# A mixture-of-experts stage whose second-layer weights are loaded from another engine's queue

## The chip, the core and the metric

The kernel runs on one core of a Trainium2 chip. The time is the device time of one execution in microseconds (us), on that core. The engines are named as in the profile: PE is TensorE (matmuls), PEld its weight loads, DVE VectorE, ACT ScalarE, POOL GpSimd, SP SyncE. A "q" behind a name means the engine's instruction queue. Any engine that issues a DMA only starts it; the bytes are moved by the core's 16 DMA engines.

## The reference, cut to what matters

Four layers follow each other on x of shape (16, 256, 256), each added to its input: attention, a gated recurrence, a mixture of four experts with a shared expert, and a recurrent net with tanh. The change touches the third alone:

```python
gate_scores = jax.nn.softmax(gate_logits, axis=-1)          # (16, 4), from means of x and the condition
topk_w, topk_i = jax.lax.top_k(gate_scores, 2)              # two experts for each of 16 images
...
for e in range(E):
    h = jax.nn.gelu(context_c @ ew1[e] + eb1[e], approximate=True)     # 256 -> 1024
    y = h @ ew2[e] + eb2[e]                                            # 1024 -> 256
    out = out + w_be[:, e][:, None, None] * mask[e][None, :, None] * y
shared = jax.nn.gelu(context_c @ sw1 + sb1, approximate=True) @ sw2 + sb2
```

## The kernel before

The kernel runs its stages one after the other, each a block with a program for every engine and a barrier at its end. During attention all expert weights are split into a high and a low part (matmuls in a fast fp32 format need both) and written to a buffer in HBM, `weight_halves` (`halves` in the code). There an expert has a 2 MB half for the first layer (w1) and one for the second (w2), laid out so that each of the 128 partitions reads one run of 16 KB.

The expert stage (`experts`, from L931) computes only what is chosen: two experts for each of 16 images are `JOBS` = 32 jobs. VectorE works out the choice, and writes the experts' numbers to the tile `which` (L1076). A job `n` has eight ticks (`FC` = 8), one for each 128 of the 1024 hidden columns. In a tick TensorE does an "up" (L1184 to L1186, six matmuls with w1 into `ph`), ScalarE the GELU (L1023), VectorE splits the result into a high part (L1131) and a low part (L1133), and two ticks later TensorE does the "down" (L1200 to L1202, six matmuls with w2 into `py`). The ups and downs are interleaved as up(t), down(t-2); a job has 96 matmuls of 256 columns.

The weights lie in two buffers each, used in turn (`n % 2`), with a semaphore for each buffer in `w_in`. The order is set by waits written by hand:

- SP reads the expert's number into a register, waits until the downs of job n-2 are done (`down_done`), and issues both loads of job n, w1 first (L950). They stand in one DMA queue.
- TensorE waits for w1 of job n before its first up (L1179) and for w2 before its first down (L1193), which comes two ticks later.
- After the last job but one SP also loads the shared expert's weights, as job 32, for the next stage. That stage (`shared_and_rnn`) begins on POOL with three memsets (L1407, L1408, L1410); TensorE waits for the last of them and for both loads (L1341) before L1296.

POOL writes a few small tables at the start of the expert stage and then waits at its end.

Of the kernel before, what the change touches and what calls it, by code (L numbers as in the profile page):

```python
# [18 lines left out]
NE, F = 4, 1024  # L19
FC = F // P  # L20
# [80 lines left out]
def build(nc, x_tok, x_dm, small_in, mod_w, w_qkv, w_out, w_fih, ew1, ew2, sw1, sw2, wx, wh, out):  # L101
# [13 lines left out]
    with hold:  # L115
        XT = sb(hold, "XT", [P, DC, B, T])
        small = sb(hold, "small", [P, SMALL_W])
        ident = sb(hold, "ident", [P, P])
        silu = sb(hold, "silu", [P, DC, B])
        eps8 = sb(hold, "eps8", [P, 1])  # L120
        wx_sb = sb(hold, "wx_sb", [P, DC, D])
        wh_sb = sb(hold, "wh_sb", [P, DC, D])
        later_loaded = sem(hold, "later_loaded")
        pieces_out = [sem(hold, f"pieces_out{q}") for q in range(2)]
        halves = nc.dram_tensor("weight_halves", (NE + 1, 2, P, 2, DC * F), fp32).ap()

        def vec(name, a=None, z=None):
            at = SMALL_AT[name]
            width = dict(SMALL)[name]
            return small[:, at + (a or 0):at + (width if z is None else z)]  # L130

        with ExitStack() as early:
            wfih_sb = sb(early, "wfih_sb", [P, DC, 3 * D])
            attention(nc, locals())
            recurrence(nc, locals())
        experts(nc, locals())
# [790 lines left out]
PIECES = 8 * (NE + 1)  # L927
# [3 lines left out]
def experts(nc, env):  # L931
    fp32, fp32r, ALU, ACT, AX = (env[k] for k in ("fp32", "fp32r", "ALU", "ACT", "AX"))
    sb, ps, sem, vec = (env[k] for k in ("sb", "ps", "sem", "vec"))
    XT, silu, halves = (env[k] for k in ("XT", "silu", "halves"))
    int32 = mybir.dt.int32
    JOBS = TOP * B
# [3 lines left out]
    with st:  # L940
        xhi = sb(st, "xhi", [P, DC, B, T], fp32r)
        xlo = sb(st, "xlo", [P, DC, B, T], fp32r)
        w1 = sb(st, "w1", [P, 2, 2, DC, F], fp32r)
        w2 = sb(st, "w2", [P, 2, 2, FC, D], fp32r)
        w_in = [[sem(st, f"w{w}_in{q}") for q in range(2)] for w in (1, 2)]

        def load_weights(sp, n, src):

            for w, dst, form in ((0, w1, "p v c f -> p (v c f)"), (1, w2, "p v c d -> p (v c d)")):
                sp.dma_start(dst[:, n % 2].bitcast(fp32).rearrange(form), src[:, w].rearrange("o p v n -> p (o v n)"))\  # L950
                    .then_inc(w_in[w][n % 2], 16)

        with ExitStack() as routed:
            g = sb(routed, "g", [P, RING, T])
# [18 lines left out]
            which = sb(routed, "which", [P, JOBS], int32)  # L973
# [8 lines left out]
            up_done, gelu_done, hi_done, lo_done, down_done, y_added, y_part = (sem(routed, n) for n in (  # L982
                "up_done", "gelu_done", "hi_done", "lo_done", "down_done", "y_added", "y_part"))
            gate_in, gate_mm, exp_in, exp_done, tables, chosen_ready, b1_ready, x_hi, x_split, biased = (
                sem(routed, n) for n in ("gate_in", "gate_mm", "exp_in", "exp_done", "tables", "chosen_ready", "b1_ready", "x_hi",
                                         "x_split", "biased"))
# [2 lines left out]

            @block.sync  # L990
            def _(sp):
                for q in range(2):
                    sp.wait_ge(env["pieces_out"][q], 16 * (PIECES // 2))
                sp.wait_ge(chosen_ready, 1)
                for n in range(JOBS):
                    e = sp.value_load(which[0:1, n:n + 1], min_val=0, max_val=NE - 1)
                    if n >= 2:
                        sp.wait_ge(down_done, FC * (n - 1))
                    load_weights(sp, n, halves[bass.ds(e, 1)])
                sp.wait_ge(down_done, FC * (JOBS - 1))  # L1000
                load_weights(sp, JOBS, halves[NE:NE + 1])

            @block.gpsimd
            def _(pool):
                nc.gpsimd.memset(ones[:], 1.0).then_inc(tables, 1)
                nc.gpsimd.memset(earlier[:], 0.0).then_inc(tables, 1)
                for e in range(NE):
                    nc.gpsimd.memset(number[:, e:e + 1], float(e)).then_inc(tables, 1)
                pool.wait_ge(tables, 2 + NE)
                for e in range(1, NE):  # L1010
                    nc.gpsimd.memset(earlier[:, e, 0:e], 1.0).then_inc(tables, 1)

            @block.scalar
            def _(act):
# [473 lines left out]
```

## Time and profile before

| | |
|---|---|
| Median of 3 runs | 1654.78 us (1653.81 to 1656.48) |
| The profiled execution | 1659.2 us |
| Its span, first to last instruction | 1657.6 us |
| Busy share of the span: PE, PEld, DVE, ACT, POOL | 79%, 62%, 52%, 39%, 20% |
| Weight loads `w<-weight_halves` | 66 of 2048 KB, median 12.0 us from issue to landing |
| Granted TensorE clock, mean | 0.890 of 2.4 GHz |

The profile is of one execution. A view by windows gives each engine's busy time within a stretch; "DMA share" is the mean busy share of the 16 DMA engines. In the timeline a row has its start and length, the engine, the line, the operation and its tiles, and in brackets how long the engine stood idle before it and what the profile takes to have ended that. A DMA's row on SP is only the issue; "DMA to landing" tells how long after the issue its data were there. "Issue" as a cause means that the profile shows nothing that the engine waited for.

### The profile page before, as it was taken

To read this page: it belongs to the slowest core of one execution; us is meant where nothing else is said; L and a number is where in the kernel's file an instruction comes from. 1 tells how busy PE (TensorE), PEld (TensorE's weight loads), DVE (VectorE), ACT (ScalarE), POOL (GpSimd) and SP (SyncE) were. 2 spreads that over 40 slices of the span, in tenths; PEclk is the share of its full clock that TensorE was granted. 3 is DMA by queue.
4 is the path that set the end of the run, shared out by engine and by line. 5 is a ranking of instruction groups with operands and counts; after the bars stand their busy time and mean duration, and the time that the engine had idled before them with its cause. 6 is when DMAs were issued, how large, how long until landed. Compare 5 with 4: busy or idle time off the path is not lost. (4 is left out here: it accounts for less than half of the span.)

```text
span 1657.6 us, 37130 instructions
## 1 busy us (share of the span) xinstructions
PE 1313.8 (79%) x15240; PEld 1035.8 (62%) x15240; DVE 855.8 (52%) x1946; ACT 645.3 (39%) x1205; POOL 324.6 (20%) x311
## 2 busy tenths in 40 slices
PE   2378887887888755445149999999998999999997
PEld 2245655655656422112049999999998888888885
DVE  3656556556555245555565565655654334433432
ACT  1155565565554445544413233323322233223332
POOL 2252342442433134444300000000000000000000
PEclk8589898898897887777559999999999999999998
DMA  8112112112112300000047888888883000000000
GB/s 320 53 39 78 39 38 77 38 39 77 39 39 77 102 0 0 0 0 0 0 203 305 340 347 334 340 353 326 345 335 125 9 16 15 16 10 16 16 15 16
DMA packets 37880, 188.06 MB, mean 113 GB/s; under 512 B 3056, under 2 KB 13424, under 8 KB 29040
## 3 DMA queue, kind: packets, MB, share of 16 engines
q1 hardware_dynamic: 37744, 186.10, 29.4%
q8 instruction: 103, 1.69, 0.4%
q14 instruction: 33, 0.27, 0.1%
HBM read 160.66 MB, written 25.17 MB: 112 GB/s over the span
## 5 line engine op out<-in xcount | busy, mean ns | idle before, releaser
L1023 ACT ACTIVATE g<-ph,b 128x256 f32<-128x256 f32 x256 | 121.5, 475 | 276.5 <-PE ph L1186 276.4
L813 PE MATMUL pg<-XT,wfih_sb 128*128 x192 | 117.6, 777 | 102.8 <-DVE logs L898 101.0
L546 DVE TENSOR_REDUCE mx<-pR 128x4 f32<-128x1024 f32 x128 | 155.6, 1222 | 70.9 <-PE pR L673 69.6
L1376 DVE STREAM_TRANSPOSE preT<-pr 128x64 f32<-128x64 f32 x256 | 64.1, 250 | 223.8 <-PE pr L1274 223.8
L1200 PE MATMUL py<-ghi,w 128*128 128x256 f32 x512 | 147.5, 288 | 20.5 <-issue 16.2
L437 ACT ACTIVATE probs<-pR 128x1024 f32<-128x1024 f32 x128 | 131.7, 1030 | 77.0 <-PE pR L682 76.8
L1184 PE MATMUL ph<-xhi,w 128*128 128x256 f32 x512 | 146.5, 286 | 17.9 <-DMA w<-weight_halves 17.9
L1131 DVE CAST ghi<-g 128x256 fp32r<-128x256 f32 x256 | 74.8, 292 | 156.8 <-ACT g L1023 156.6
L813 PEld LDWEIGHTS pg<-XT,wfih_sb 128*128 128x128 f32 x192 | 47.4, 257 | 172.8 <-issue 172.8
L1350 ACT ACTIVATE hs<-preT 128x32 f32<-128x32 f32 x256 | 58.8, 230 | 228.6 <-DVE preT L1376 228.6
L1185 PE MATMUL ph<-xlo,w 128*128 128x256 f32 x512 | 146.0, 285 | 0.0
L1186 PE MATMUL ph<-xhi,w 128*128 128x256 f32 x512 | 145.9, 285 | 0.0
L1201 PE MATMUL py<-glo,w 128*128 128x256 f32 x512 | 145.3, 284 | 0.0
L1202 PE MATMUL py<-ghi,w 128*128 128x256 f32 x512 | 145.3, 284 | 0.0
L1274 PE MATMUL pr<-wh_sb,hs 128*32 128x64 f32 x4096 | 112.1, 228 | 15.5 <-ACT hs L1350 15.5
L1200 PEld LDWEIGHTS py<-ghi,w 128*128 128x128 f32 x512 | 98.6, 192 | 25.3 <-DVE glo L1133 14.0
L1133 DVE TENSOR_TENSOR glo<-g,ghi 128x256 fp32r<-128x256 f32 x256 | 109.0, 426 | 8.8
L1184 PEld LDWEIGHTS ph<-xhi,w 128*128 128x128 f32 x512 | 99.4, 194 | 18.9 <-issue 17.2
L673 PE MATMUL pR<-KT,QT 48*128 48x256 f32 x512 | 62.1, 332 | 57.1 <-DVE mx L546 56.8
L1274 PEld LDWEIGHTS pr<-wh_sb,hs 128*32 128x32 f32 x4096 | 70.1, 110 | 50.6 <-ACT hs L1350 20.9
L1186 PEld LDWEIGHTS ph<-xhi,w 128*128 128x128 f32 x512 | 99.4, 194 | 0.0
L1185 PEld LDWEIGHTS ph<-xlo,w 128*128 128x128 f32 x512 | 99.4, 194 | 0.0
(189 smaller groups left out, 3006.5 us busy)
## 6 DMA issues: line engine op xcount, KB each, us to landing
w<-weight_halves SPq DMA_DIRECT2D x66, 2048.0 KB, 12.0
weight_halves<-wparts SPq DMA_DIRECT2D x40, 512.0 KB, 4.0
modw<-in_ew SPq DMA_DIRECT2D x32, 256.0 KB, 4.3
xn<-in_x_tok SPq DMA_DIRECT2D x4, 1024.0 KB, 12.0
XT<-in_x_dm SPq DMA_DIRECT2D x2, 2048.0 KB, 14.0
out_dm<-staged SPq DMA_DIRECT2D x16, 256.0 KB, 2.1
modw<-in_sw SPq DMA_DIRECT2D x8, 256.0 KB, 4.2
modw<-in_mod_w SPq DMA_DIRECT2D x1, 768.0 KB, 7.4
```

What stands on the lines that cost most here:

```text
L437: nc.scalar.activation(probs[:, j % 4], pR[k][:], ACT.Exp, scale=HD ** -0.5).then_inc(free[k], 1)
L546: nc.vector.reduce_max(mx[:, :, 2 * j:2 * j + 2].rearrange("p t s -> p s t"), pR[k][:].rearrange("p s (t k) -> p s t k", t=TC), AX.X).then ...
L813: i = nc.tensor.matmul(pg[u][:, g], wfih[:, c, g * D + u * P:g * D + (u + 1) * P], XT[:, c, bass.ds(2 * p, 2)], start=(c == 0), stop=(c == ...
L1023: nc.scalar.activation(g[:, t % RING], ph[t % RING][:, 0:T], ACT.Gelu_apprx_tanh, bias=b1[:, n, f:f + 1]).then_inc(gelu_done, 1)
L1133: nc.vector.tensor_tensor(glo[:, t % RING], g[:, t % RING], ghi[:, t % RING].bitcast(fp32), ALU.subtract).then_inc(lo_done, 1)
L1184: nc.tensor.matmul(dst, whi, hi, start=(k == 0), stop=False)
L1185: nc.tensor.matmul(dst, whi, lo, start=False, stop=False)
L1186: i = nc.tensor.matmul(dst, wlo, hi, start=False, stop=(k == DC - 1))
L1200: nc.tensor.matmul(dst, whi, hi, start=(f == 0), stop=False)
L1201: nc.tensor.matmul(dst, whi, lo, start=False, stop=False)
L1202: i = nc.tensor.matmul(dst, wlo, hi, start=False, stop=(f == FC - 1))
L1274: i = nc.tensor.matmul(dst[QW * j:QW * (j + 1)], prev[:, c], quad(wh[:, c], j), start=False, stop=(c == DC - 1), skip_group_check=True)
```

## The change

`load_weights` loads one of the two layers, and a new helper `load_all` holds the loop that SP had. SP calls it for w1, POOL for w2, behind its small tables. Each of the two engines waits for the stored halves and for the choice, reads the expert's number for each job and waits for `down_done` with the same values as before. The semaphores that TensorE waits for are the same.

```diff
-        def load_weights(sp, n, src):
-            for w, dst, form in ((0, w1, "p v c f -> p (v c f)"), (1, w2, "p v c d -> p (v c d)")):
-                sp.dma_start(dst[:, n % 2].bitcast(fp32).rearrange(form), src[:, w].rearrange("o p v n -> p (o v n)"))\
-                    .then_inc(w_in[w][n % 2], 16)
+        def load_weights(eng, n, src, w):
+            dst, form = ((w1, "p v c f -> p (v c f)"), (w2, "p v c d -> p (v c d)"))[w]
+            eng.dma_start(dst[:, n % 2].bitcast(fp32).rearrange(form), src[:, w].rearrange("o p v n -> p (o v n)"))\
+                .then_inc(w_in[w][n % 2], 16)
+
+        def load_all(eng, w, which, chosen_ready, down_done):
+            for q in range(2):
+                eng.wait_ge(env["pieces_out"][q], 16 * (PIECES // 2))
+            eng.wait_ge(chosen_ready, 1)
+            for n in range(JOBS):
+                e = eng.value_load(which[0:1, n:n + 1], min_val=0, max_val=NE - 1)
+                if n >= 2:
+                    eng.wait_ge(down_done, FC * (n - 1))
+                load_weights(eng, n, halves[bass.ds(e, 1)], w)
+            eng.wait_ge(down_done, FC * (JOBS - 1))
+            load_weights(eng, JOBS, halves[NE:NE + 1], w)
...
             @block.sync
             def _(sp):
-                for q in range(2):
-                    sp.wait_ge(env["pieces_out"][q], 16 * (PIECES // 2))
-                sp.wait_ge(chosen_ready, 1)
-                for n in range(JOBS):
-                    e = sp.value_load(which[0:1, n:n + 1], min_val=0, max_val=NE - 1)
-                    if n >= 2:
-                        sp.wait_ge(down_done, FC * (n - 1))
-                    load_weights(sp, n, halves[bass.ds(e, 1)])
-                sp.wait_ge(down_done, FC * (JOBS - 1))
-                load_weights(sp, JOBS, halves[NE:NE + 1])
+                load_all(sp, 0, which, chosen_ready, down_done)
...
             @block.gpsimd
             def _(pool):
...
+                load_all(pool, 1, which, chosen_ready, down_done)
```

## Rows read from the trace of the kernel before

**Rows 1.** Window: us; busy of PE, PEld, DVE, ACT, POOL; clock, DMA share, GB/s.

```profile
873.40:1246.40 373.00, 351.63 (x2882) 346.86 (x2880) 220.66 (x643) 114.00 (x240) 0.00 (x0) 1.00 0.85 339
```

**Rows 2.** Timeline of SP's queue: first and last weight loads of the steady part.

```profile
873.37 0.85 SPq L950 DMA_DIRECT2D w<-weight_halves  x2
...
1246.35 0.34 SPq L950 DMA_DIRECT2D w<-weight_halves  x1
```

**Rows 3.** Timeline of TensorE within a job.

```profile
1226.01 0.28 PE L1184 MATMUL ph<-xhi,w 128*128 128x256 f32 x1
1226.13 0.28 PE L1185 MATMUL ph<-xlo,w 128*128 128x256 f32 x1
```

**Rows 4.** Waits from 873.4 to 1246.4 us: total us, times, longest.

```profile
PE py L1200 <- issue: 15.6, 19, 1.3
...
PE ph L1184 <- DMA w<-weight_halves: 2.5, 3, 1.4
```

**Rows 5.** Timeline and landing (L950): job 13's w1, its w2, TensorE's next start.

```profile
1010.44 0.34 SPq L950 DMA_DIRECT2D w<-weight_halves  x1
...
DMA to landing us min/median/max: 7.7/7.7/7.7
...
1010.96 0.33 SPq L950 DMA_DIRECT2D w<-weight_halves  x1
...
DMA to landing us min/median/max: 12.1/12.1/12.1
...
1023.13 0.35 PE L1200 MATMUL py<-ghi,w 128*128 128x256 f32 x1 [0.64 <-issue]
```

**Rows 6.** Windows in and after the body of a job's loads.

```profile
1013.50:1022.00 8.50, 8.50 (x74) 8.50 (x73) 6.62 (x21) 2.85 (x6) 0.00 (x0) 1.00 0.99 422
1022.00:1024.50 2.50, 1.86 (x16) 1.69 (x15) 1.08 (x3) 0.47 (x1) 0.00 (x0) 1.00 0.67 164
```

**Rows 7.** Timeline and landing (L950): job 30's w1, TensorE's stop, the next issue.

```profile
1220.59 0.34 SPq L950 DMA_DIRECT2D w<-weight_halves  x1
...
DMA to landing us min/median/max: 9.7/9.7/9.7
...
1228.77 0.28 PE L1202 MATMUL py<-ghi,w 128*128 128x256 f32 x1
1230.47 0.35 PE L1184 MATMUL ph<-xhi,w 128*128 128x256 f32 x1 [1.42 <-DMA w<-weight_halves]
...
1233.75 0.85 SPq L950 DMA_DIRECT2D w<-weight_halves  x2
```

**Rows 8.** Timeline of POOL around the stage.

```profile
1258.77 1.80 POOL L1407 MEMSET hs<- 128x2048 f32 x1 [433.51 <-POOLq L953]
```

**Rows 9.** DMA transfers from 873.4 to 1246.4 us.

```profile
DMA packets 8673, 126.29 MB, mean 339 GB/s; under 512 B 959, under 2 KB 959, under 8 KB 959
```

**Rows 10.** Timeline of TensorE before the last stage, and the window after it.

```profile
1260.90 0.58 PE L1296 MATMUL phs<-xhi,w 128*128 128x256 f32 x1 [3.45 <-POOL row L1410]
1261.28 0.42 PE L1298 MATMUL phs<-xlo,w 128*128 128x256 f32 x1
1261.49 0.41 PE L1300 MATMUL phs<-xhi,w 128*128 128x256 f32 x1
...
1260.12:1266.92 6.80, 6.02 (x28) 6.02 (x29) 2.34 (x7) 1.43 (x3) 0.67 (x3) 0.50 0.00 0
```

**Rows 11.** Landing (L950) and timeline: job 0's w1 and the first matmul.

```profile
L950 SPq DMA_DIRECT2D w<-weight_halves x1: 378/378/378, 846.7 to 846.7; - x1
...
DMA to landing us min/median/max: 7.9/7.9/7.9
...
854.70 0.55 PE L1184 MATMUL ph<-xhi,w 128*128 128x256 f32 x1 [15.33 <-DMA w<-weight_halves]
```

**Rows 12.** The page, part 5: VectorE's two operations on the hidden layer.

```profile
L1131 DVE CAST ghi<-g 128x256 fp32r<-128x256 f32 x256 | 74.8, 292 | 156.8 <-ACT g L1023 156.6
...
L1133 DVE TENSOR_TENSOR glo<-g,ghi 128x256 fp32r<-128x256 f32 x256 | 109.0, 426 | 8.8
```

## The prediction

> **What bounds the kernel now.** I read the span by stages first. The expert stage, from the first weight load at 846.7 us [rows 11] to the end of the last expert at about 1257 us, is the only one that the change touches; its steady part alone is 373.00 us [rows 1]. In that stretch TensorE is busy 351.63 us, the clock is granted in full, GpSimd does nothing and the 16 DMA engines are busy 0.85 of the time at 339 GB/s. Two resources are therefore near their limit at once, and what counts is which one is late at which point.
>
> The queue of SP says how long one job (one chosen expert of one image) takes: the loads for job 2 are issued at 873.37 us, those for the shared expert, which stand in as job 32, at 1246.35 us [rows 2]. That is 30 periods in 372.98 us, 12.43 us each. A job has 96 matmuls, one every 0.12 us [rows 3], so TensorE needs 11.52 us; the other 0.91 us, 27 us over the stage, is waiting. The list of waits shows where: before L1200, the first matmul that reads the second layer's weights (w2), 15.6 us in 19 stops are put down to "issue"; before L1184, which reads the first layer's (w1), a DMA costs 2.5 us in 3 stops [rows 4].
>
> One job shows what "issue" hides. Its w1 load is issued at 1010.44 and lands 7.7 us later; its w2 load is issued 0.52 us behind it and lands after 12.1 us, thus at 1023.04. TensorE stands idle and goes on at 1023.13 [rows 5], 0.09 us after the landing, though ScalarE and VectorE had nothing left to deliver for that matmul (the page names an engine because it has no better candidate). So **w2's landing is what is late now, by about one microsecond in a typical job, and w1's is not, or hardly**. The reason that w1 is early is order: both loads stand in one queue, so w1's 2 MB go through the DMA engines first. In the body of a load the engines are busy 0.99 of the time at 422 GB/s [rows 6]: they are full, and 2.10 MB take 4.97 us there. The difference of the two landings, 1023.04 less 1018.14, is 4.9 us, the same thing.
>
> **When is each load due?** The job in which w1 was late gives this without arithmetic on ticks. Its load was issued at 1220.59 and took 9.7 us, to 1230.3. TensorE's last matmul before the stop began at 1228.77; the next could have begun at 1228.89, 8.3 us after the issue. It began at 1230.47, and the next pair of loads went out at 1233.75 [rows 7], 3.4 us after the landing, since 24 matmuls and the semaphore stand between them. So when w1 decides, the period is w1's time to landing plus 3.4 us, and it decides from 8.1 us on (8.1 + 3.4 = 11.5). w2 is due 30 matmuls, 3.6 us, after w1's point: at 11.9 us after the issue.
>
> **The change, part by part.**
>
> (a) Removed from SP: one of two DMA issues per job (0.34 us) and its address registers. SP only waits between them, so this is worth nothing by itself. The SP queue holds nothing else in this stage.
>
> (b) Added to POOL: three waits, 32 reads of the expert's number, 33 DMA issues. POOL is idle from 825 to 1258 us [rows 8], and the read stands ahead of the wait for L1202, as on SP. Behind the load loop on POOL stand only the block's end and the memset L1407; the last load goes out near 1246.35 and L1407 starts at 1258.77, when the other engines have reached the block's end, so 12 us cover it. Cost zero; without that cover it would be once the issue, below 1 us.
>
> (c) Moved: w2's transfer leaves the queue in which it stood behind w1's. Both sets of 2.10 MB now ask for the same 16 DMA engines at almost the same time. Nothing in this trace has two bulk queues active at once, nor any DMA issued by POOL, so I bound the delay of w1. Lower end zero: POOL's load starts only when w1's is through, or yields to it. Upper end 4.9 us: w2 goes wholly ahead. If the engines serve both queues in turn, w1 waits for as many of w2's packets as it has itself left when these begin to come: 4.9 us less POOL's extra start-up. The nearest row for a start-up is the 0.52 us between two issues on SP; POOL may need two or three times that. The packets of this stage are 16.4 KB each [rows 9], so a load is 8 packets on each engine, 0.6 us apiece; who comes last in a turn is half of one, 0.3 us. With 1 us of start-up the delay is 4.9 - 1.0 - 0.3, about 3.5 us. I take that: it lies nearest to the row for a start-up, and nothing in the trace gives either side precedence. w1's own time is 7.7 us in the typical job and 9.7 in the late one [rows 5, 7]; I take 8.0 as an average. So w1 lands after 11.5 us.
>
> The Trainium skill says the same of the engines ("DMA: Bandwidth & Descriptors", Queues, rings and completion order): each serves in turn the queues that hold work for it, a packet at a time. No row of before can show it; by that rule alone the sum is the one I make. The same page gives software-generated DMAs from GpSimd a first byte after about 1 us against 0.6 us for SP's; with their difference of 0.4 us as start-up the delay would be, as an estimate, 4.2 us, and the sum 21 us higher.
>
> (d) Period by w1: 11.5 + 3.4 = 14.9 us. The stop before L1184 is then 3.4 us long in every job, where TensorE stands idle. w2, landing after some 12.6 us as now (the engines have the same bytes to move), is due 14.9 + 0.7 us after the issue and is no longer late.
>
> (e) The clock. A stop of TensorE that ends at 1260.90 us, 3.45 us idle, is followed by a granted clock of 0.50, the 1.2 GHz level, for 6.8 us, with matmuls 0.21 us apart [rows 10]; the stop of 1.42 us at 1230.47 did not lower it [rows 7], since the steady part's mean is 1.00 [rows 1]. The new stops are as long as the first. If the clock is down for all 24 matmuls between w1's landing and the next issue, the period grows by 24 x (0.213 - 0.12) = 2.2 us; if never, by zero. Slow matmuls elsewhere in the job only shorten the stop. I take the middle, 1.1 us: the fall comes some way into or after the stop, so that it covers part of those 24.
>
> (f) Start and end. w1 of job 0 goes out at 846.71, lands 7.9 us later and releases TensorE at 854.70 [rows 11]. It now shares with w2 of job 0: +3.5 us, less the 0.5 us for which job 1 waited for w2. End: the last stage waits for both loads of the shared expert, issued at 1246.35, but it starts at 1260.90 behind L1407 and L1410 [rows 8, 10], 14.5 us after the issue; both land within 12.9 us. Zero.
>
> **Sum.** Period 11.5 + 3.4 + 1.1 = 16.0 us against 12.43: 3.57 x 30 = 107 us. With 3 us at the start: +110 us. The profiled execution took 1659.2 us (span 1657.6), 4.4 us above the median of the three timed runs, 1654.78; the sum is a difference, so I put it on the median: **1765 us, 6.6% slower**.
>
> **A second rule, against the change.** The cast L1131 takes 0.29 us for 256 elements, the two-input L1133 0.42 us [rows 12], so the cast is the quicker of the two at one size. The Trainium skill ("SBUF — State Buffer", the "DVE blocks DMA" trap) says that while VectorE runs a copy in its two-port mode, as casts of this kind are, GpSimd can't write descriptors for its DMAs. No row here shows it. As an estimate it would start w2 up to 0.29 us later and let w1 keep that much more of the engines: up to 9 us less than the sum, in the direction of rival 1.
>
> **The rivals.**
>
> 1. *w1 keeps its lead, w2 is late instead* (18%). If POOL's start-up is long (3 us and more) or its queue yields, w1 is hardly delayed and every microsecond by which w2 lands later than its present 12.6 us is paid directly. For: POOL generates nothing in this trace, so its start-up is unbounded by rows. Against: it would have to be six times SP's 0.52 us. With 0.5 to 1.5 us on each of 30 jobs (15 to 45 us): 1670 to 1700 us.
>
> 2. *w2 goes ahead of w1* (13%). Delay 4.9 us and w1 at 12.9 us: period 16.3 without and 18.5 us with the full loss of clock: +116 to +182 us, with 5 us at the start 1775 to 1842 us.
>
> 3. *Faster* (4%). Two queues keep the engines busy across the gap between jobs, where they were only 0.67 busy [rows 6], and w2 lands by 11.9 us while w1 still lands by 8.1. That removes the 0.91 us: 1627 us. It decides from the point where 4.19 MB land within 11.9 us; at 422 GB/s they take 9.9 us, and a load's own latency is 7.7 - 4.9 = 2.8 us, 12.7 together. So the gap would have to yield 0.8 us.
>
> 4. *No change* (4%): SP's queue is served first and w2's packets follow at once from the other, as they did behind w1 in one queue, so that w2 lands at 12.6 us as before. 1655 us.
>
> The forecast case has 61%, with its own range from 1705 (delay 2.5 us, period 13.9 and little loss of clock: +45 us and 2 to start, raised by a fall now and then) to 1815 us (delay 4.2 and the full 2.2 us).
>
> **How the numbers follow.** Below 1670 lie rivals 3 and 4, 8%; above 1825 the upper third of rival 2, 4%. The range leaves out these 12%: 1670 to 1825. A difference under 0.2% (3.3 us, about what can be told from no change here) comes from rival 4: 4%. Faster 4%, slower 92%.
>
> **What the new profile would show.** Right: a stop before L1184 in nearly every job, by DMA, 3 us long, some 100 us in all; the stops before L1200 gone; issues near 16 us apart; w1 landing after 11 to 12 us and w2 close behind; the granted clock of 873 to the stage's end between 0.75 and 0.95; DMA share down to about 0.66 (0.85 x 12.43 / 16.0). Wrong: w1 still landing within 8.5 us (rival 1, 3 or 4, told apart by w2's landing); w1 landing last (rival 2); or a clock of 1.00 in spite of the stops, which would take (e), 33 us, out of the sum and leave 1732 us.

## The result and the profile after

The changed kernel takes 1734.28 us (median of 4 runs, 1732.15 to 1738.73), the kernel before 1654.30 us beside it (1653.65 to 1656.48). The ratio is 1.0485, with an interval of 1.0459 to 1.0510: slower by 80 us. The profiled execution took 1732.15 us with a span of 1730.5 us, 72.9 us more than the span of before; the rest of the 80 is how the single runs lie (the profiled one is the fastest of the changed kernel, and the profiled one of the kernel before, 1659.2 us, lies above its four timed runs).

The windows of the expert stage first: from the first to the last load of its steady part, from there to the next stage, and one stretch of 3.3 us inside. The columns are those of [rows 1].

```profile
875.60:1316.20 440.60, 368.13 (x2882) 362.92 (x2881) 221.31 (x643) 113.69 (x240) 15.84 (x30) 0.96 0.72 287
1316.20:1332.00 15.80, 10.17 (x84) 9.84 (x82) 6.60 (x20) 2.84 (x6) 1.19 (x2) 0.88 0.68 267
1068.95:1072.25 3.30, 3.30 (x17) 3.30 (x17) 1.41 (x4) 0.73 (x2) 0.00 (x0) 0.50 0.00 0
```

The steady part has grown from 373.0 to 440.6 us. The engines of DMA are less busy (0.72 for 0.85) and move 287 instead of 339 GB/s: the same bytes in more time, with pauses. The clock, 1.00 before, is 0.96, since stretches like the one at 1068.95 ran at 0.50, the 1.2 GHz level. The period follows from the queue of SP, as in [rows 2]:

```profile
875.56 0.34 SPq L950 DMA_DIRECT2D w<-weight_halves  x1
...
1316.15 0.34 SPq L950 DMA_DIRECT2D w<-weight_halves  x1
```

(1316.15 - 875.56) / 30 = 14.69 us, against 12.43. Who waits now (total us, times, longest)?

```profile
POOL w L950 <- PE py L1206: 436.7, 30, 27.2
...
PE ph L1188 <- DMA w<-weight_halves: 72.5, 30, 3.9
```

What answers to [rows 4] has turned round: the stops before the matmul that reads w2 are gone from the list, and there is one of 2.4 us in each of the 30 jobs before L1188, which reads w1 and was L1184. The landings of both loads over the steady part (minimum, median, maximum after the issue):

```profile
L950 SPq DMA_DIRECT2D w<-weight_halves x31: 337/338/347, 875.6 to 1316.1; - x31
...
DMA to landing us min/median/max: 10.0/10.5/12.2
...
L950 POOL DMA_DIRECT2D w<-weight_halves x31: 527/527/530, 876.0 to 1316.4; - x31
...
DMA to landing us min/median/max: 12.0/12.5/13.6
```

w1, which came 7.7 us after its issue in the typical job of [rows 5], now takes 10.5. The mean over the 30 loads, from the records of their landings, is 10.77 us, and 8.14 before. w2 is as late after w1's issue as it was, 13.2 us (13.4 before). One job in detail, by the timeline:

```profile
1113.38 0.34 SPq L950 DMA_DIRECT2D w<-weight_halves  x1
...
1113.86 0.53 POOL L950 DMA_DIRECT2D w<-weight_halves  x1 [13.03 <-PE py L1206]
...
1121.56 0.28 PE L1206 MATMUL py<-ghi,w 128*128 128x256 f32 x1
1123.64 0.35 PE L1188 MATMUL ph<-xhi,w 128*128 128x256 f32 x1 [1.81 <-DMA w<-weight_halves]
...
1126.92 0.34 SPq L950 DMA_DIRECT2D w<-weight_halves  x1
```

w1 goes out at 1113.38 and lands 10.1 us later, at 1123.5; TensorE, free since 1121.83, goes on 0.1 us after that, and the next load goes out 3.4 us after the landing, as in [rows 7]. Which queue moved data in that job is in the view of the DMA queues (packets, MB, share of the 16 engines), read for three stretches: 0 to 4 us after the issue, 4.6 to 8.6 us, 10.1 to 12.6 us.

```profile
q1 hardware_dynamic: 59, 0.97, 75.8%
...
q0 software_dynamic: 54, 0.88, 51.6%
q1 hardware_dynamic: 54, 0.88, 51.6%
...
q0 software_dynamic: 52, 0.59, 55.4%
```

First SP's queue q1 alone (POOL's q0 has no row there), then 54 packets from each, then POOL's alone. The engines take turns packet by packet, and a 16 KB packet takes 0.61 us, as before. By the packet records of 30 jobs, POOL's first packet moves 3.6 us after SP's first, and SP's load has started 75 of its 128 packets by then. The first 16 of a load take 1.29 us each in the mean in both kernels, the later ones 0.61: so these 75 are what 3.6 us hold, and not the 94 that they would hold at the later pace. At the stage's end the barrier's drains are new:

```profile
L965 POOLq DRAIN  x1: 14694/14694/14694, 1316.4 to 1316.4; - x1
...
L965 DVEq DRAIN  x1: 1031/1031/1031, 1326.4 to 1326.4; - x1
```

POOL's queue drains for 14.69 us, from 1316.4 to 1331.1, while VectorE is through at 1327.45. L1411 (L1407 before) must wait for that, and TensorE stands idle for 7.10 us instead of the 3.45 of [rows 10]:

```profile
1331.34 1.80 POOL L1411 MEMSET hs<- 128x2048 f32 x1 [14.39 <-POOLq L965]
...
1333.47 0.58 PE L1300 MATMUL phs<-xhi,w 128*128 128x256 f32 x1 [7.10 <-POOL row L1414]
```

The next stage thus starts 17.3 us after the last issue, 14.5 before. The difference of the spans is accounted for: 2.2 us up to the loads of job 2, 67.6 us in 30 periods, 2.8 us at the stage's end and 0.3 us after it, together 72.9.

### The profile page after: what moved, and what is told of

Same layout as the page of the kernel before. It is cut to its first block and busy times, and to the rows that moved or that the text cites. A ratio compares the mean times of both kernels' runs of the same rounds, so it can differ in the third digit from the quotient of the medians.

```text
span 1730.5 us, 37229 instructions
## 1 busy us (share of the span) xinstructions
PE 1331.9 (77%) x15240; PEld 1050.8 (61%) x15240; DVE 856.2 (49%) x1946; ACT 644.6 (37%) x1205; POOL 342.0 (20%) x344
## 3 DMA queue, kind: packets, MB, share of 16 engines
q1 hardware_dynamic: 32992, 116.90, 18.7%
## 5 line engine op out<-in xcount | busy, mean ns | idle before, releaser
L1188 PE MATMUL ph<-xhi,w 128*128 128x256 f32 x512 | 152.4, 298 | 90.2 <-DMA w<-weight_halves 90.2
L1188 PEld LDWEIGHTS ph<-xhi,w 128*128 128x128 f32 x512 | 103.5, 202 | 95.7 <-issue 95.7
L1204 PE MATMUL py<-ghi,w 128*128 128x256 f32 x512 | 148.9, 291 | 2.1 <-DMA w<-weight_halves 1.1
L1190 PE MATMUL ph<-xhi,w 128*128 128x256 f32 x512 | 148.8, 291 | 0.0
L1206 PE MATMUL py<-ghi,w 128*128 128x256 f32 x512 | 148.7, 290 | 0.0
L950 POOL DMA_DIRECT2D w<-weight_halves x33 | 17.7, 535 | 474.2 <-PE py L1206 451.7
L1189 PEld LDWEIGHTS ph<-xlo,w 128*128 128x128 f32 x512 | 103.4, 202 | 0.0
L1190 PEld LDWEIGHTS ph<-xhi,w 128*128 128x128 f32 x512 | 102.8, 201 | 0.0
## 6 DMA issues: line engine op xcount, KB each, us to landing
w<-weight_halves SPq DMA_DIRECT2D x33, 2048.0 KB, 10.5
XT<-in_x_dm SPq DMA_DIRECT2D x2, 2048.0 KB, 13.8
```

Source lines behind the costliest of these rows:

```text
L1188: nc.tensor.matmul(dst, whi, hi, start=(k == 0), stop=False)
L1189: nc.tensor.matmul(dst, whi, lo, start=False, stop=False)
L1190: i = nc.tensor.matmul(dst, wlo, hi, start=False, stop=(k == DC - 1))
L1204: nc.tensor.matmul(dst, whi, hi, start=(f == 0), stop=False)
L1206: i = nc.tensor.matmul(dst, wlo, hi, start=False, stop=(f == FC - 1))
```

## The experiments

Two theories stood against each other after this. **S**: two transfers that are in the engines together take turns, so that the one that is needed first is late, and how late depends on the head start. **P**: a DMA from POOL is itself the cost, whoever shares with it. The ratios are those to the kernel before, run beside each.

| kernel | median us | ratio (interval) | period us | w1 lands, mean us | w1's landing to next issue, mean us | clock in the steady part |
|---|---|---|---|---|---|---|
| before | 1654.30 | 1 | 12.43 | 8.14 | 4.29 | 1.00 |
| changed | 1734.28 | 1.0485 (1.0459 to 1.0510) | 14.69 | 10.77 | 3.92 | 0.96 |
| held_2 | 1676.51 | 1.0123 (1.0097 to 1.0148) | 12.96 | 8.34 | 4.62 | 0.99 |
| both_pool | 1672.43 | 1.0110 (1.0093 to 1.0127) | 12.72 | 8.29 | 4.43 | 1.00 |
| act_queue | 1837.43 | 1.1098 (1.1080 to 1.1117) | 18.34 | 13.08 | 5.26 | 0.86 |
| swapped | 1843.58 | 1.1140 (1.1122 to 1.1159) | 18.32 | 12.60 | 5.72 | 0.86 |
| sp_later | 1866.10 | 1.1266 (1.1233 to 1.1299) | 19.28 | 12.41 | 6.87 | 0.85 |
| warm | 1710.49 | 1.0328 (1.0312 to 1.0344) | 14.08 | 10.67 | 3.41 | 1.00 |
| last_on_sp | 1727.38 | 1.0440 (1.0419 to 1.0461) | 14.45 | 10.67 | 3.78 | 0.97 |
| early_sp | 1627.72 | 0.9824 (0.9811 to 0.9838) | 11.55 | 8.09 | | 1.00 |
| early_two | 1636.63 | 0.9886 (0.9866 to 0.9906) | 11.64 | 10.24 | | 1.00 |

The last three columns and the period are over jobs 2 to 31 of the profiled execution, from its records; w1's landing and the time from it to the next issue add up to the period (where w2 is late, its stop lies in the second). In `swapped` the second also holds the 0.47 us by which POOL's issue comes behind SP's, in `sp_later` the tick by which SP waits longer. In the two last kernels w1's load no longer waits for the same event, so that column says nothing there.

**held_2: the overlap taken away, POOL kept.**

```diff
+        held = 2
...
                 if n >= 2:
-                    eng.wait_ge(down_done, FC * (n - 1))
+                    eng.wait_ge(down_done, FC * (n - 1) + held * w)
...
-            eng.wait_ge(down_done, FC * (JOBS - 1))
+            eng.wait_ge(down_done, FC * (JOBS - 1) + held * w)
```

> The changed kernel, but POOL issues each w2 load two ticks (about 2.9 us) later than w1's. Theory S (the two transfers take turns on the DMA engines, and w1 is late by the time in which w2's packets come between its own): w2's packets begin when w1's are nearly through, so w1 lands after about 8.2 us instead of 10.8, w2 at about 13 us after w1's issue, the stop before L1188 all but vanishes, the period is 12.5 to 12.9 us, and the time 1655 to 1672 us. Theory P (a DMA from POOL is itself the cost, by software descriptors or slower packets, whoever shares with it): no gain or a loss, 1735 us or more, since w2 only starts later.

Measured: 1676.51 us. w1's landings as in the view above:

```profile
L950 SPq DMA_DIRECT2D w<-weight_halves x31: 337/338/347, 875.2 to 1264.0; - x31
...
DMA to landing us min/median/max: 7.6/7.8/12.2
```

Their median is 7.8 us, and 58 us of the 80 are gone with w2 issued 4.45 us after w1 in the mean. That is more than the two ticks, since TensorE's stop for w2 lies between them. P falls as the main cause. The time is 4 us above what I expected of S: w2 lands 14.1 us after w1's issue and is now itself late, and the next stage starts only 18.7 us after the last issue of w1, since the last w2 goes out 3.8 us after it and POOL's drain waits for its landing.

**both_pool: POOL's queue alone.** `load_all` issues both layers, w1 first, on POOL; SP has none.

```diff
-        def load_all(eng, w, which, chosen_ready, down_done):
+        def load_all(eng, ws, which, chosen_ready, down_done):
...
-                load_weights(eng, n, halves[bass.ds(e, 1)], w)
+                for w in ws:
+                    load_weights(eng, n, halves[bass.ds(e, 1)], w)
...
-                load_all(sp, 0, which, chosen_ready, down_done)
...
-                load_all(pool, 1, which, chosen_ready, down_done)
+                load_all(pool, (0, 1), which, chosen_ready, down_done)
```

> Both loads issued by POOL, w1 first, in its one queue, none by SP. Theory S: no sharing, only POOL's own start-up, about 2 us over SP's: w1 lands after 10.1 us, w2 some 4.9 us behind it, period about 13.5 us, time 1690 us with 3 us at the stage's end. If the start-up were nothing and all were sharing: 1655 to 1660 us. Theory P: as slow as the changed kernel or slower, 1735 us and up.

Measured: 1672.43 us, period 12.72. w1 lands after 8.29 us, only 0.15 us later than from SP. The 2 us of start-up over SP's that I had given POOL for this run don't exist when it is alone. The kernel's span is 12.6 us longer than before, 9 of them in the periods and 5 at the stage's end (19.3 us for 14.5), less 1 in the last stage. In the 4 us after an issue (1077.14, w1 of job 18) POOL's queue moves 64 packets, 56 of them large, where SP's moved 59 in the changed kernel's job above:

```profile
DMA packets 64, 0.92 MB, mean 229 GB/s; under 512 B 8, under 2 KB 8, under 8 KB 8
...
q0 software_dynamic: 64, 0.92, 72.0%
```

The steady part's window is close to the one of before [rows 1], with POOL busy 31.65 us for 61 issues:

```profile
873.70:1255.40 381.70, 352.53 (x2876) 346.62 (x2875) 220.62 (x643) 113.43 (x240) 31.65 (x61) 1.00 0.84 331
```

**act_queue: the same overlap without POOL.** ScalarE issues the w2 loads between its GELUs, behind the same wait for `down_done`. The cut shows the loop; ahead of it ScalarE waits for the stored halves and the choice and loads w2 of jobs 0 and 1.

```diff
...
+                    if f == 1 and 2 <= n + 1 < JOBS:
+                        e = act.value_load(which[0:1, n + 1:n + 2], min_val=0, max_val=NE - 1)
+                    if f == 2 and 2 <= n + 1 <= JOBS:
+                        act.wait_ge(down_done, FC * n)
+                        load_weights(act, n + 1, halves[bass.ds(e, 1)] if n + 1 < JOBS else halves[NE:NE + 1], 1)
...
-                load_all(pool, 1, which, chosen_ready, down_done)
```

> w2 loaded from ScalarE's queue in place of POOL's, at the same point. Theory S: ScalarE's DMAs are generated like SP's, so w2 loses the late start that it had on POOL (about 2 us) and w1 has to share from its first packet: w1 lands after 12.3 to 12.9 us, period 15.8 to 17 us, time 1755 to 1790 us, slower than with POOL. Theory P (POOL's software path is the cost): back to about 1655 us.

Measured: 1837.43 us, slower than with POOL and above my range for S. This is S in its pure form: the two issues are less than 0.01 us apart in the mean (0.49 in the changed kernel), and in the first 4 us after the issue at 1172.55 each queue has its part:

```profile
q1 hardware_dynamic: 35, 0.57, 46.4%
q10 hardware_dynamic: 30, 0.49, 31.7%
```

w1's landings (its line is L950 there too):

```profile
L950 SPq DMA_DIRECT2D w<-weight_halves x31: 337/338/346, 876.8 to 1426.9; - x31
...
DMA to landing us min/median/max: 12.0/13.0/13.9
```

13.08 us in the mean is the whole of w2's transfer, 4.9 us, on top of 8.14. The rest of the period is the clock, at 0.86 over the steady part:

```profile
876.80:1426.90 550.10, 409.59 (x2881) 404.38 (x2880) 221.37 (x643) 114.04 (x240) 0.00 (x0) 0.86 0.57 230
```

With stops of up to 5.4 us, the 24 matmuls between the landing and the next issue took 5.26 - 3.41 = 1.85 us more than at the full clock, near the bound of 2.2 that (e) of the prediction gives. It is slow in all 30 jobs (4.68 us or more).

**swapped: w1 on POOL, w2 on SP.**

```diff
-                load_all(sp, 0, which, chosen_ready, down_done)
+                load_all(sp, 1, which, chosen_ready, down_done)
...
-                load_all(pool, 1, which, chosen_ready, down_done)
+                load_all(pool, 0, which, chosen_ready, down_done)
```

> w1 loaded from POOL's queue and w2 from SP's. Theory S: now w1 is the one that starts late and shares: it lands last, after about 13 us, as w2 does in the changed kernel; period 16.5 us by that alone and up to 17.7 with a lowered clock; time 1775 to 1815 us. A theory in which only the number of queues counted and not which load starts first: 1734 us as before.

Measured: 1843.58 us. The two queues behave as in the changed kernel, with the tensors exchanged; the medians of the landings are within 0.1 us of those above:

```profile
L950 SPq DMA_DIRECT2D w<-weight_halves x31: 337/338/347, 880.7 to 1430.6; - x31
...
DMA to landing us min/median/max: 10.1/10.4/11.7
...
L950 POOL DMA_DIRECT2D w<-weight_halves x31: 527/527/530, 881.2 to 1430.9; - x31
...
DMA to landing us min/median/max: 12.1/12.4/13.4
```

SP's load is early again, but it is the wrong one: what counts is whether the load that is due first is also the one whose data start first. It came out 29 us above my range. From w1's landing to its next issue 5.72 us pass, 2.31 over the shortest value; 0.47 of them are POOL's issue, which comes that much behind SP's, and 1.84 are left for the clock, as in `act_queue`.

**sp_later: who comes second waits.** SP waits one tick more, so that POOL's load goes out first.

```diff
             if n >= 2:
-                eng.wait_ge(down_done, FC * (n - 1))
+                eng.wait_ge(down_done, FC * (n - 1) + 1 - w)
...
-            eng.wait_ge(down_done, FC * (JOBS - 1))
+            eng.wait_ge(down_done, FC * (JOBS - 1) + 1 - w)
```

> The changed kernel, but SP issues w1 one tick (1.4 us) after POOL issues w2. In the changed kernel POOL's first packet moves only 4.1 us after its issue, with POOL alone in both_pool 1.2 us after. If the difference is that the engines are already full with SP's packets, POOL's first packet comes here after 1.2 to 1.5 us. If it is something that POOL's DMA always pays beside SP, it stays at 4 us. Slower as a kernel: w1 lands last, 1800 us or more.

Measured: 1866.10 us, by two runs, 1865.96 and 1866.23. One job's issues, and the queues from just after the first of them to 4.75 us behind it:

```profile
1185.25 0.53 POOL L950 DMA_DIRECT2D w<-weight_halves  x1 [18.52 <-PE py L1206]
...
1186.33 0.34 SPq L950 DMA_DIRECT2D w<-weight_halves  x1
```

```profile
q0 software_dynamic: 74, 1.21, 74.8%
```

SP's queue q1 has no row in that stretch, though its load was issued 3.7 us before the stretch's end. By the packet records, over 30 jobs: POOL's first packet moves 1.2 us after its issue and SP's 3.9 us after. In the changed kernel it is the other way round, SP's after 1.0 us and POOL's after 4.1. The head start in issue is 0.49 us in the changed kernel, 0.47 in `swapped` and 0.99 here; in data it is 3.6 us in all three, and the first load has started 75 of its 128 packets in all three. So it isn't a start-up of POOL's. Which part of the engines holds the second queue back for that long is not shown.

**warm: the clock's part.**

```diff
                     pe.wait_ge(x_split, n // TOP + 1)
+                    if n >= 2:
+                        for _ in range(15):
+                            nc.tensor.matmul(ph[t % RING][:, 0:T], xhi[:, 0, n // TOP, 0:P], xhi[:, 0, n // TOP], start=True, stop=True)
                     pe.wait_ge(w_in[0][n % 2], 16 * (n // 2 + 1))
```

> The changed kernel with 15 more matmuls (1.8 us at 0.12 us each) from job 2 on, ahead of TensorE's wait for w1; they write into the bank that the next matmul starts anew. They fill the idle stop (never under 1.8 us in the changed kernel) without lengthening it. Theory: the lowered clock costs what lies between w1's landing and the next issue over its shortest value: 3.92 - 3.41 = 0.5 us a job. Then the clock stays at 1.00, the period falls from 14.69 to 14.2 us, and the time by 15 us, to about 1719 us. If the clock's fall cost nothing (it only eats into the stops): 1734 us.

Measured: 1710.49 us, 24 us less than the changed kernel, with 450 matmuls more.

```profile
875.20:1297.70 422.50, 408.15 (x3331) 402.37 (x3330) 221.23 (x643) 114.02 (x240) 15.86 (x30) 1.00 0.76 299
```

The clock is back at 1.00 and the mean from landing to issue is 3.41 us, the value without a lowered clock: 0.51 us a job or 15 us are the clock's. The mean hides two kinds of jobs. In the changed kernel 19 of the 30 intervals from w1's landing to the next issue last 3.42 to 3.45 us, the other 11 last 4.54 to 5.16. The length of the stop alone doesn't tell which: a w1 that landed after 11.6 us was followed by 3.42 us, one after 10.1 us by 4.54. The other 9 us were not expected. Of the 21.2 us between the two spans, 15 are the clock's, 3 are w1's landing (10.67 for 10.77), 1 the stage's end and 2 the last stage; whether the clock has a part in the last three stays open. The remaining 3 us of the medians' 24 are not in the two profiled executions.

**last_on_sp: the stage's end.** The load of job 32's w2 goes from SP, with a semaphore of its own, for which TensorE then waits.

```diff
+        last_in = sem(st, "last_in")
...
-            eng.wait_ge(down_done, FC * (JOBS - 1))
-            load_weights(eng, JOBS, halves[NE:NE + 1], w)
+            if w == 0:
+                eng.wait_ge(down_done, FC * (JOBS - 1))
+                load_weights(eng, JOBS, halves[NE:NE + 1], 0)
+                eng.dma_start(w2[:, JOBS % 2].bitcast(fp32).rearrange("p v c d -> p (v c d)"), halves[NE:NE + 1, 1].rearrange("o p v n -> p (o v n)"))\
+                    .then_inc(last_in, 16)
...
-                pe.wait_ge(ex["w_in"][w][BUF], 16 * (TOP * B // 2 + 1))
+                pe.wait_ge(ex["w_in"][w][BUF], 16 * (TOP * B // 2 + 1 - w))
+            pe.wait_ge(ex["last_in"], 16)
```

> The changed kernel, but the one load of the shared expert's w2 is issued by SP behind w1's, with a semaphore of its own; the other 32 stay on POOL. Theory: POOL's drain at the end of the stage lasts until its own last DMA is through (14.69 us in the changed kernel), and holds the next stage back. Then POOL's drain ends at once, the next stage starts 14.5 us after the last issue as before, not 17.3, and the time falls by 3 us, to 1731 us. If something else holds the stage's end, 17.3 us stay.

Measured: 1727.38 us; its runs spread from 1720.86 to 1732.28 and touch those of the changed kernel, so the profile has to decide. From SP's last w1 issue to the next stage's first matmul:

```profile
1308.87 0.34 SPq L952 DMA_DIRECT2D w<-weight_halves  x1
...
1322.66 0.55 PE L1305 MATMUL phs<-xhi,w 128*128 128x256 f32 x1 [3.57 <-POOL row L1420]
```

13.8 us, not 17.3, and the idle time of TensorE is 3.57 us, not 7.10: 3.5 us of the span are the stage's end. The periods (14.45 us for 14.69) give another 7 us in this execution, the fastest of the four; nothing in the edit touches them, so I don't count them. POOL's drain there ended at 1309.4, 1.4 us after POOL's own last load landed; in the changed kernel that interval is 1.4 us as well (landing 1329.7, end 1331.1).

**early_sp and early_two: the overlap used well.** w1's buffer is free when the ups of job n-2 are done, five groups of matmuls before the downs are. In `early_sp` (from the kernel before) SP waits for that before w1 and for the downs before w2; in `early_two` (from the changed kernel) SP does so for w1 and POOL loads w2.

```diff
-        def load_weights(sp, n, src):
+        def load_weights(sp, n, src, free):
...
+                if n >= 2:
+                    sp.wait_ge(free[w], FC * (n - 1))
...
-                    if n >= 2:
-                        sp.wait_ge(down_done, FC * (n - 1))
-                    load_weights(sp, n, halves[bass.ds(e, 1)])
+                    load_weights(sp, n, halves[bass.ds(e, 1)], (up_done, down_done))
```

The edit above is `early_sp`'s; that of `early_two` is one word, besides a parameter of `load_all` that is renamed:

```diff
-                load_all(sp, 0, which, chosen_ready, down_done)
+                load_all(sp, 0, which, chosen_ready, up_done)
```

> The kernel before (both loads on SP's one queue), but w1's load of job n waits only until the ups of job n-2 are done, which is five groups of six matmuls, 3.6 us, before the downs are; w2's waits as before. The two transfers follow each other in one queue and start while the last w2 still lands. If my account of the due times is right, w1 lands before its due time and w2 before 11.9 us, no stop is left, the period falls from 12.43 to TensorE's 11.52 us, and the time by 27 us, to 1627 us. If the engines' 9.9 us of transfer per job and their start-up can't be packed into 11.52 us, the period stays above 12.

Measured: 1627.72 us, 0.9824 of the kernel before. Steady part and all of TensorE's waits in it:

```profile
867.80:1214.20 346.40, 345.94 (x2882) 345.74 (x2882) 222.15 (x648) 113.50 (x241) 0.00 (x0) 1.00 0.92 364
```

```profile
PE py L1199 <- DVE glo L1132: 0.5, 1, 0.5
```

TensorE is busy 345.94 of 346.40 us: the period is its 96 matmuls. This is the fastest of all kernels here.

> The same early w1 load in the changed kernel: SP loads w1 when the ups of job n-2 are done, POOL w2 when the downs are. w1 now has 3.6 us of lead by issue, so that little is left to share: w1 lands in time, w2's packets follow. Theory S: the loss is an overlap in time, so it vanishes: period 11.5 to 11.6 us, 1627 to 1632 us. Rival (two queues or POOL cost something by themselves): a period over 12 us, 1650 us and more.

Measured: 1636.63 us, 0.9886 of the kernel before and 98 us less than the changed kernel, by one wait of SP.

```profile
871.00:1220.20 349.20, 347.74 (x2882) 346.20 (x2882) 222.45 (x648) 113.55 (x240) 15.84 (x30) 1.00 0.95 360
```

The period, 11.64 us, is what S foretells, though w1 still lands late after its issue (10.6 us in the median): issued 3.6 us earlier, it isn't due before 3.6 + 8.1 = 11.7 us. By the packet records, 112 of w1's 128 packets start within 0.3 us of their times in the kernel before, and the last one 8.8 us after the issue, not 6.5; w2's have begun by then. The time is 5 us above the range; POOL's drain costs part of it (it ends 2.2 us after VectorE's), 3 us lie in the periods against `early_sp`'s, 3 us in the first two jobs.

## Why the prediction came out as it did

The direction, the main mechanism (the two loads take turns, and w1 is late) and the turn of the waits were right; the size was 1765 us for 1734, +110 for +80, of which the two profiled executions show 72.9. Two terms of the sum were too large, the delay of w1 and the clock; they erred in the same direction and did not cancel. Inside the delay two errors did cancel in part, as (c) below shows, and that the term came as near as it did is luck.

- **Bound and due times** held. w1 decides above 8.1 us and its landing is followed by the next issue after 3.4 us; `warm` measures 3.41, and `early_sp`, with a period of 11.55 us, shows that the 0.91 us of each period were waits for the loads.
- **(a), (b)** cost nothing in the periods, as said: POOL's issue follows SP's by 0.49 us, where SP's own second one followed the first by 0.52. (b) missed one thing, at the end.
- **(c), w1 at 11.5 us**, was mis-sized: 10.77, so 0.73 us a job and 22 us in the sum too many. The delay is 2.63 us (10.77 less 8.14) and not 3.5. The turns are there (54 packets each), but two parts of the term were wrong. The head start in data is 3.6 us, not 1, and it isn't POOL's start-up: alone POOL's w1 lands 0.15 us after SP's (`both_pool`), and behind POOL SP is held back as long (`sp_later`). And w1's transfer doesn't run at an even pace: its first packets are slow, so that 53 of 128 are left after those 3.6 us. By the sum's own formula the true head start would have given 4.9 - 3.6 - 0.3 = 1.0 us. The 53 packets at 0.61 us on 16 engines make 2.0 us; the last one starts 2.4 us later than in the kernel before, which is most of the 2.63. The rest stays open.
- **(d)** w2 is no longer late: right, no stop on it is left in the list.
- **(e), 1.1 us for the clock**, was mis-sized as well: 0.5 us a job, 18 us in the sum. The middle of the bounds stood for a fall that covers part of the 24 matmuls in every job; in fact 11 of 30 jobs paid 1.1 to 1.7 us and 19 nothing. That the stops are 2.4 us and not 3.4 goes with it: where they are 4.7 us every job paid, 1.85 us in the mean in `act_queue` and 1.84 in `swapped`, within the bound of 2.2. The mean clock of 0.96 lies above the 0.75 to 0.95 that I named.
- **(f)** The start was 2.2 us for 3. The end was not zero but 2.8 us: the 12 us of cover named in (b) were too short, since POOL's drain waits for its own DMA. `last_on_sp` removes it.
- In sum: 110 - 22 (w1) - 18 (clock) - 1 (start) + 3 (end) = 72 us, the profile's 72.9.
- **The rivals.** Rival 1's condition was met and its outcome wasn't: w2's data start 3.6 us after w1's, beyond the 3 us that it asked for, and still w1 lands 2.6 us late, while w2 lands 13.2 us after w1's issue, 13.4 before. Rival 4 is out, since w1 and not w2 decides. Rival 2 (w1 lands last) is what `swapped` made, and `act_queue` nearly (w1 after 13.08 us, w2 after 13.24): +183 and +189 us, where its upper end was 1842 us, +187. Rival 3 is false for this kernel: the gap between jobs stays. Its idea works where w1's load is issued before the last w2 has landed, in `early_sp` and `early_two`. The first-byte times of the Trainium skill ("DMA: Bandwidth & Descriptors", Specifications: about 1 us for GpSimd's, 0.6 for SP's) agree with POOL undisturbed and SP undisturbed in their order (1.24 and 0.97 us from the start of the issue to the first packet); the 0.4 us between them is 0.27 here, and 0.15 by the landings. The rule of turns at packets in the Trainium skill ("DMA: Bandwidth & Descriptors", Queues, rings and completion order) is what the 54 packets from each queue show.
- The rule of the Trainium skill that VectorE's copies in two-port mode keep GpSimd from writing descriptors ("SBUF — State Buffer", the "DVE blocks DMA" trap) left no mark that these runs can show: POOL's issue takes 0.53 us in each of the 31 loads of the view above, with casts running throughout, and w1 from POOL alone is 0.15 us slower than from SP.

## What to carry to other kernels

Two loads that are due at different times and issued at the same time are best put in one queue, in the order of their due times. On two queues they took turns here, and the load that was due first was delayed by 2.6 us with its data first, and by 4.9 us, the whole length of the second, when both started together. Before loads are spread over queues, look at what each waits for: here the gain lay in freeing the first buffer earlier, worth 29 us with one queue, and 98 us of the changed kernel with two. And when a DMA moves to POOL, look for POOL's drain at the next barrier: here it lasted until that DMA had landed.

## What the runs showed of the hardware that was not expected

- A load that is issued while another queue's load is starting gets its first packet 4 us after its issue, not after 1.0 to 1.2. It holds for POOL behind SP (4.1 us) and for SP behind POOL (3.9 us), with the issues 0.5 to 1 us apart: 3.6 us between the first packets, 75 of 128 packets of the first load, in `after` (the changed kernel), `swapped` and `sp_later`. With POOL's issue 4.45 us behind (`held_2`) its first packet came 2.1 us after the issue in the mean (1.2 to 3.3). ScalarE's, issued in the same moment as SP's, had its first packet after 1.9 us in the mean. After that the queues share evenly.
- The first 16 packets of a 2 MB load took 1.29 us each in the mean, the later ones 0.61 us.
- POOL's drain at a block's end ran on to 1.4 us past the landing of POOL's last DMA (in the changed kernel, `last_on_sp`, `warm`, `swapped`, `held_2`, `early_two` and `sp_later`), and 2.7 us past it in `both_pool`, where POOL had issued both loads; SP's took 0.13 us with its own load still in flight.
- A lowered clock cost far more with longer stops: stops of 2.4 us left a mean of 0.96 and slow matmuls in 11 of 30 jobs, stops of 4.7 us (`act_queue`) 0.86 and slow matmuls in all 30.
